# Graph-attention scores computed on quarters of TensorE and summed by VectorE, instead of on halves of TensorE

## The chip, the cores and the metric

The kernel runs on one NeuronCore of one Trainium2 chip. The metric is the device time of one execution in microseconds (us). TensorE (PE in the profile) multiplies matrices, VectorE (DVE), ScalarE (ACT) and GpSimd (POOL) work on elements, and SyncE (SP) issues most of the transfers. PEld is TensorE's loading of weights, which runs beside its products.

## The reference, cut to what matters

There are 128 graphs of 64 nodes with 384 features. For each graph the scores of all node pairs are computed, masked where `adj` has no edge, and normalised by a softmax; with these weights the rows are averaged, go through two dense layers, and are added to the input, and each row is normalised.

```python
hi_t = jnp.einsum('bid,de->bie', h, W1_w[:HID])[:, :, None, :] + jnp.einsum('bijd,de->bije', dep_emb, W1_w[HID:]) + W1_b
hj_t = jnp.einsum('bjd,de->bje', h, W2_w[:HID])[:, None, :, :] + jnp.einsum('bijd,de->bije', dep_emb, W2_w[HID:]) + W2_b
relevance = jnp.sum(hi_t * hj_t, axis=-1)
masked = jnp.where(adj, relevance, NEG)
A = jax.nn.softmax(masked, axis=2)
aggregated = jnp.einsum('bij,bjd->bid', A, h_syn)
h_syn = jax.nn.relu(aggregated @ gcn_w + gcn_b)
return h_syn @ Wo_w + Wo_b          # then x = layernorm(x + this)
```

Where all entries of `adj` are 0 or 1, as here, the score of nodes i and j is a product of two 384-long vectors plus a term of the row.

## The kernel before, in words

The 8192 nodes are cut into 16 groups (`GROUPS`; `LAST` is 15) of 512 tokens. A group is 4 pairs of graphs (`PAIRS`), and a pair fills the 128 partitions: graph e of a pair has partitions 64e to 64e+63. The 384 features are 3 blocks of 128 (`C`). Each engine has its own program, written by hand; `run` executes `body(g, par)` for g = 0 and 1, then in a loop for 2 to 13, then for 14 and 15. The engines wait for each other through counted semaphores alone, and each works strictly in the order of its program. PSUM has 8 banks, given out by hand.

TensorE's `body(g)` does, in this order:

- `mix(g - 1)`: the weighted sums of group g-1, 48 products on 64x64 quarters of the array, into banks 4 to 7. It waits for the turned weights `at_sb` (`at_ready`, from VectorE) and until ScalarE has read the latest projections out of PSUM (`gt_ready`). Its middle is marked by `mix_part`.
- `score_stage(g)`: the scores, 24 products per group, each with all 128 rows of the array and 64 of its columns (graph e on column half e), three blocks c accumulated into bank 0.
- `gemm(g - 1)`: the first dense layer, 27 products of 128x512 into three banks (`GEMM_BANK`), each value in a high and a low part. It waits for the split input (`zlo`) and for the bank to be read (`added`).
- `proj(g + 1)`: the projection for the next scores, again 27 products of 128x512.
- `out(g - 1, q)`, q = 0 to 3: the second dense layer, 9 products of 128x384 for each pair. The first waits for all three low parts of the hidden layer, `hslo`, and in group 1 also for `wo_lo`, which GpSimd computes once.

VectorE's `body(g)` does: `low_z(g - 1)` (six subtractions that give `z_lo`, after ScalarE's `z_hi`); then the score stage: `rel` from the scores in PSUM, the row term `srow` and `adj_sb`, the addition of `neg_sb`, and `nmax`, the negated row maximum; then `most` (`adj_max`). It waits for ScalarE's exponentials (`weigh`, which waits for `nmax`), and continues with `rsum`, `weights`, `turn` (`at_sb`, which releases `at_ready`), `row_products` of the next group (`onehot`, `xu_row`), `normalise` of group g-2, `low_hidden(g - 1)` (three operations that give `hs_lo` and release `hslo`), and `residual(g - 1, q)`, which reads the second layer out of PSUM (`added`).

GpSimd does the large element-wise work of SBUF alone: `split_x` (`xt_lo`), `bias_x` (`y_sb`), and once `wo_lo`, for which it waits until `row_products` of group 2 are there (`xu_ready`). ScalarE's `body(g)` is `split_z`, in group 1 `row_terms` and `split_x`, `weigh`, `hidden`, `split_x` of a later group, and `project_out`.

Of the kernel before, what the change touches and what calls it, by code (L numbers as in the profile page):

```python
# [41 lines left out]
ALU = mybir.AluOpType  # L42
# [4 lines left out]
P = 128  # L47
# [6 lines left out]
def gnn_layernorm_kernel(nc, x, x_t, adj, adj_t, edge, biases, w1_t, w2_t, gcn_w, wo_w, wo_b, out):  # L54
    HID, TOKENS = x_t.shape
    NODES = adj.shape[2]
    EDIM, NTYPES = edge.shape[0], edge.shape[1] - 2 * HID
    C = HID // P
    PAIRS = 4
    GT = PAIRS * P  # L60
    GROUPS = TOKENS // GT
    HALVES = PAIRS // 2
    MIX = PAIRS * NODES
    LAST = GROUPS - 1
# [14 lines left out]
    with ExitStack() as ctx:  # L79
# [3 lines left out]
        def sem(name):  # L83
            return ctx.enter_context(nc.semaphore(name))
# [34 lines left out]
        xt_sb = sb("xt_sb", [P, 2, C, GT])  # L119
# [52 lines left out]
        banks = ctx.enter_context(nc.psum_tensor("banks", [P, 8, 512], F32))  # L172
        bank = [banks[:, i, :] for i in range(8)]
        score = bank[0]
        GEMM_BANK = [bank[2], bank[3], bank[1]]
        PROJ_BANK = bank[4:7]
        PROJ1_BANK = bank[1:4]
        M_BANK = bank[4:7]
        U_BANK = bank[7]
        C_BANK = bank[3]  # L180
# [67 lines left out]
        mix_part = sem("mix_part")  # L248
        xu_ready = sem("xu_ready")
        srow_ready = sem("srow_ready")  # L250
        masked = sem("masked")
        expd = sem("expd")
        normed = sem("normed")
# [59 lines left out]
        def out_bank(g, q):  # L313

            if static(g, LAST - 2) and HALVES <= q:
                return bank[(3, 2)[q - HALVES]]
            if static(g, LAST - 1):
                return bank[(3, 1, 6, 7)[q]]
            if static(g, LAST):
                return bank[(3, 1, 2, 4)[q]]  # L320
            return bank[(1, 2, 3, 1)[q]]

        def gemm_bank(g):

            return [bank[2], bank[4], bank[5]] if static(g, LAST) else GEMM_BANK

        def column(g, q):

# [32 lines left out]
        def static(g, n):  # L361

            return isinstance(g, int) and g == n
# [96 lines left out]
        def _(pe):  # L460
# [6 lines left out]
            def proj(g, par, into=PROJ_BANK, parts=range(C * C)):  # L467

                for part in parts:
                    f, c = part // C, part % C  # L470
                    fs = slice(f * P, (f + 1) * P)
                    mm = three(into[f][:, 0:GT], m_hi[:, c, fs], m_lo[:, c, fs],
                               xt_hi[:, par, c, :], xt_lo[:, par, c, :], c == 0, c == C - 1)
                    if c == C - 1:
                        mm.then_inc(proj_mm, 1)

            def score_stage(g, par):
                pe.wait_ge(gt_ready, C * (g + 1))
                for n in range(PAIRS):
                    for c in range(C):  # L480
                        for e in range(2):
                            ts = slice(n * P + e * NODES, n * P + (e + 1) * NODES)
                            mm = pe.matmul(score[e * NODES:(e + 1) * NODES, n * NODES:(n + 1) * NODES],  # L483
                                           gt_sb[:, c, ts], xt_sb[:, par, c, ts], start=(c == 0), stop=(c == C - 1))
                mm.then_inc(score_mm, 1)

            def gemm(g):

                for f in range(C):
                    fs = slice(f * P, (f + 1) * P)  # L490
                    if static(g, LAST):
                        pe.wait_ge(added, PAIRS * (g - 1))
                    elif not (static(g, 0) or static(g, LAST - 1) and f == C - 1):
                        pe.wait_ge(added, PAIRS * (g - 1) + f + 2)
                    for n, c in enumerate(BLOCKS):
                        if f == 0:
                            pe.wait_ge(zlo, C * g + n + 1)
                        mm = three(gemm_bank(g)[f][:, 0:GT], gcn_hi[:, c, fs], gcn_lo[:, c, fs],
                                   z_hi[:, c, :], z_lo[:, c, :], n == 0, n == C - 1)
                    mm.then_inc(gemm_mm, 1)  # L500

            def mix(g, par):
                pe.wait_ge(at_ready, g + 1)
                if static(g, 0):
                    pe.wait_ge(gt_ready, C)
                elif not static(g, LAST):
                    pe.wait_ge(gt_ready, C * (g + 2))
                pe.sem_inc(mix_begun, 1)

                def pass_of(*streams):  # L510

                    for q in range(PAIRS):
                        for f, h in streams:
                            at = MIX * (f % 2)
                            rows = slice(h * NODES, (h + 1) * NODES)
                            for e in range(2):
                                mm = pe.matmul(  # L517
                                    bank[MIX_BANK[h][f]][e * NODES:(e + 1) * NODES, at + q * NODES:at + (q + 1) * NODES],
                                    x_sb[rows, par, q, f * P + e * NODES:f * P + (e + 1) * NODES],
                                    at_sb[rows, q * NODES:(q + 1) * NODES], start=True, stop=True)  # L520
                    return mm

                pass_of((0, 1), (0, 0))
                pass_of((1, 1), (1, 0)).then_inc(mix_part, 1)
                pass_of((2, 1), (2, 0)).then_inc(mix_mm, 1)
# [81 lines left out]
            def body(g, par):  # L607

                if not static(g, 0):
                    mix(g - 1, 1 - par)  # L610
                score_stage(g, par)
                if static(g, 0):
                    proj(1, 1, PROJ1_BANK, range(2, C * C))
                    return
                if static(g, 1):
                    pe.wait_ge(gcn_lo_ready, 1)
                gemm(g - 1)
                if static(g, LAST):
                    out(g - 2, 3)
                    mix(g, par)  # L620
                    out(g - 1, 0)
                    out(g - 1, 1)
                    gemm(g)
                    out(g - 1, 2)
                    out(g - 1, 3)
                    for q in range(PAIRS):
                        out(g, q)
                    return
                pe.wait_ge(xlo, g + 2)
                proj(g + 1, 1 - par)  # L630
                if static(g, 1):
                    pe.wait_ge(wo_lo_ready, 1)
                for q in range(PAIRS - 1 if static(g, LAST - 1) else PAIRS):
                    out(g - 1, q)
# [191 lines left out]
        def _(dve):  # L826
# [118 lines left out]
            def body(g, par):  # L945

                if not static(g, 0):
                    low_z(g - 1)
                dve.wait_ge(score_mm, g + 1)
                dve.wait_ge(negm, g + 1)  # L950
                dve.wait_ge(srow_ready, g + 1)
                for q in range(PAIRS):
                    a = dve.scalar_tensor_tensor(rel[:, q, :], score[:, q * NODES:(q + 1) * NODES],  # L953
                                                 srow[:, q:q + 1], adj_sb[:, par, q, :], ALU.add, ALU.mult)
                a.then_inc(masked, 1)
                dve.wait_ge(masked, 3 * g + 1)
                dve.tensor_tensor(rel[:], rel[:], neg_sb[:, par], ALU.add).then_inc(masked, 1)
                dve.wait_ge(masked, 3 * g + 2)
# [283 lines left out]
```

## Time and profile before

| what | value |
|---|---|
| median of 3 runs | 376.71 us (376.21 to 377.17) |
| the profiled execution's own time | 376.19 us |
| its span, first to last instruction | 374.3 us |
| mean granted TensorE clock | 0.998 of full speed |
| PE busy | 364.7 us, 97% of the span |
| DVE busy | 274.8 us, 73% |
| ACT busy | 180.1 us, 48% |
| POOL busy | 144.9 us, 39% |

All times below are microseconds from the span's start. In a row of the timeline the first number is the start, the second the duration, then come engine, line, operation, output<-inputs, shapes and the number of instructions in it; square brackets give the idle time of that engine just before, and what ended it. An fp32 product shows as two records on TensorE, so 24 products are x48. Matmul durations include the pipeline, so neighbours overlap, and the distance between two starts is the price of one.

### The profile page before, as it was taken

How to read it: one execution, taken by the hardware profiler on the slowest of the kernel's cores; microseconds unless marked ns; L12 is line 12 of the kernel's file. 1: busy time of each engine (PE TensorE's matmuls, PEld its weight loads, DVE VectorE, ACT ScalarE, POOL GpSimd, SP SyncE). 2: the span in 40 equal slices, each digit the busy share in tenths (PEclk: the TensorE clock that was granted, in tenths of full speed). 3: DMA queues.
4: the chain of work that ended last, by engine and by line, in shares of the span. 5: the costliest groups of instructions: out<-in, count | busy, mean ns of one | idle time of the engine just before them, and what ended most of it. 6: DMA issues, size and time to landing. Idle time of an engine off the chain costs nothing.

```text
span 374.3 us, 9938 instructions
## 1 busy us (share of the span) xinstructions
PE 364.7 (97%) x3827; PEld 316.7 (85%) x3827; DVE 274.8 (73%) x773; ACT 180.1 (48%) x371; POOL 144.9 (39%) x108
## 2 busy tenths in 40 slices
PE   8999999999999999999999999999999999999994
PEld 5787798988889898888989888898988989897893
DVE  1559768687786868788686878868677785867856
ACT  1566717165272715527272552727255282616552
POOL 1603461716134171613517152351715235142714
PEclk9999999999999999999999999999999999999999
DMA  7995005564443556344354534435553443550033
GB/s 236 353 328 170 28 10 176 168 185 132 146 158 92 174 168 182 120 156 158 88 179 168 182 113 154 165 89 179 168 179 101 162 161 100 168 170 4 17 112 129
DMA packets 43268, 55.48 MB, mean 148 GB/s; under 512 B 10352, under 2 KB 37488, under 8 KB 43248
## 3 DMA queue, kind: packets, MB, share of 16 engines
q1 hardware_dynamic: 42448, 54.30, 45.8%
q10 hardware_dynamic: 800, 0.90, 0.7%
q8 instruction: 13, 0.21, 0.2%
q14 instruction: 7, 0.06, 0.1%
HBM read 42.61 MB, written 12.58 MB: 147 GB/s over the span
## 4 chain that ended last, share of the span: by engine, by line
PE 89%; DVE 7%; DMA 1%; POOL 1%; ACT 1%; issue 1%; POOLq 0%
PE banks L463 25%; PE banks L465 24%; PE banks L464 24%; PE banks L517 6%; PE banks L483 6%; PE banks L557 2%; DVE onehot L833 1%; DVE z_lo L923 1%; DMA w1t_sb<-in_w_t_dram 1%; DVE adj_max L916 1%; DVE at_sb L941 1%; POOL wo_lo L1173 1%; ACT prob L752 1%; DVE rel L953 1%; DVE at_sb L936 0%
## 5 line engine op out<-in xcount | busy, mean ns | idle before, releaser
L1128 POOL TENSOR_TENSOR y_sb<-y_sb,wob_sb 128x1536 f32<-128x1536 f32 x15 | 52.8, 3519 | 84.7 <-DVE y_sb L864 73.8
L764 ACT CAST z_hi<-banks 128x512 fp32r<-128x512 f32 x48 | 26.6, 588 | 99.3 <-PE banks L517 93.9
L842 DVE TENSOR_TENSOR y_sb<-banks,y_sb 128x384 f32<-128x384 f32 x60 | 33.4, 556 | 48.7 <-PE banks L465 44.3
L463 PE MATMUL banks<-wo_hi,hs_hi 128*128 128x384 f32 x180 | 60.7, 337 | 1.6 <-DVE xt_lo L930 1.2
L464 PE MATMUL banks<-wo_lo,hs_hi 128*128 128x384 f32 x180 | 60.5, 336 | 0.0
L465 PE MATMUL banks<-wo_hi,hs_lo 128*128 128x384 f32 x180 | 60.5, 336 | 0.0
L463 PE MATMUL banks<-z_hi,gcn_hi 128*128 128x512 f32 x144 | 58.3, 405 | 0.0
L463 PE MATMUL banks<-xt_hi,m_hi 128*128 128x512 f32 x144 | 57.2, 397 | 0.0
L465 PE MATMUL banks<-xt_hi,m_lo 128*128 128x512 f32 x144 | 56.4, 392 | 0.0
L465 PE MATMUL banks<-z_hi,gcn_lo 128*128 128x512 f32 x144 | 56.4, 392 | 0.0
L464 PE MATMUL banks<-z_lo,gcn_hi 128*128 128x512 f32 x144 | 56.1, 389 | 0.0
L464 PE MATMUL banks<-xt_lo,m_hi 128*128 128x512 f32 x144 | 56.0, 389 | 0.0
L1116 POOL TENSOR_TENSOR xt_lo<-xt_sb,xt_hi 128x1536 fp32r<-128x1536 f32 x15 | 53.1, 3538 | 7.2 <-ACT xt_hi L707 7.2
L713 ACT ACTIVATE gt_sb<-banks,r_sb 128x512 f32<-128x512 f32 x48 | 32.8, 686 | 32.6 <-PE banks L465 32.6
L1136 POOL TENSOR_TENSOR veps<-mv,eps_sb 128x4 f32<-128x4 f32 (+2 forms) x20 | 4.1, 206 | 107.4 <-DVE mv L856 107.4
L923 DVE TENSOR_TENSOR z_lo<-banks,z_hi 128x256 fp32r<-128x256 f32 x96 | 34.6, 418 | 8.3 <-ACT z_hi L764 8.3
L752 ACT ACTIVATE prob<-rel,nmax 128x64 f32<-128x64 f32 x64 | 21.5, 337 | 36.2 <-DVE nmax L959 36.2
L463 PEld LDWEIGHTS banks<-wo_hi,hs_hi 128*128 128x128 f32 x180 | 33.8, 188 | 3.0 <-DVE xt_lo L930 1.6
L847 DVE BATCH_NORM_STATS2 stats<-y_sb 128x6 f32<-128x384 f32 x60 | 33.6, 560 | 2.1
L930 DVE SCALAR_TENSOR_TENSOR hs_lo<-banks,ngb_sb,less_sb 128x512 fp32r<-128x512 f32 x45 | 31.2, 746 | 4.7 <-ACT less_sb L777 4.7
L464 PEld LDWEIGHTS banks<-wo_lo,hs_hi 128*128 128x128 f32 x180 | 33.8, 188 | 0.5
L465 PEld LDWEIGHTS banks<-wo_hi,hs_lo 128*128 128x128 f32 x180 | 33.8, 188 | 0.0
(103 smaller groups left out, 612.6 us busy)
## 6 DMA issues: line engine op xcount, KB each, us to landing
x_sb<-in_x_dram SPq DMA_DIRECT2D x16, 768.0 KB, 4.6
xt_sb<-in_x_t_dram SPq DMA_DIRECT2D x15, 768.0 KB, 6.5
y_sb<-in_x_dram SPq DMA_DIRECT2D x15, 768.0 KB, 4.5
out_dram<-y_sb SPq DMA_DIRECT2D x30, 384.0 KB, 2.5
adj_sb<-in_adj_dram SPq DMA_DIRECT2D x32, 64.0 KB, 3.1
xt_sb<-in_x_t_dram SPq DMA_DIRECT2D x2, 384.0 KB, 6.6
xt_sb<-in_x_dram SPq DMA_DIRECT2D x1, 768.0 KB, 6.1
w2t_sb<-in_w_t_dram SPq DMA_DIRECT2D x3, 192.0 KB, 4.5
```

The lines of the kernel that those rows point to most:

```text
L463: pe.matmul(acc, a_hi, b_hi, start=first, stop=False)
L464: pe.matmul(acc, a_hi, b_lo, start=False, stop=False)
L465: return pe.matmul(acc, a_lo, b_hi, start=False, stop=last)
L713: act.activation(gt_sb[:, f, :], of[f][:, 0:GT], ACT.Identity, bias=r_sb[:, f:f + 1]).then_inc(gt_ready, 1)
L752: a = act.activation(prob[:, q, :], rel[:, q, :], ACT.Exp, bias=nmax[:, q:q + 1], accum_out=psum_row[:, q:q + 1])
L764: act.copy(by_graph(z_hi[:, f, :]), mixed(f)).then_inc(zhi, 1)
L842: dve.tensor_tensor(y_home(g, slot)[:, q, :], out_bank(g, q)[:, 0:HID], y_home(g, slot)[:, q, :], ALU.add).then_inc(added, 1)
L847: dve.bn_stats(stats[:, q, :], y_home(g, slot)[:, q, :]).then_inc(statd, 1)
L923: a = dve.tensor_tensor(by_graph(z_lo[:, f, :])[:, h], mixed(f)[:, h], by_graph(f32(z_hi[:, f, :]))[:, h], ALU.subtract)
L930: dve.scalar_tensor_tensor(hs_home(g)[1][:, f, :], gemm_bank(g)[f][:, 0:GT], ngb_sb[:, f:f + 1], less_sb[:, f, :], ALU.max, ALU.subtract). ...
L1116: pool.tensor_tensor(xt_lo[:, slot], xt_sb[:, slot], f32(xt_hi[:, slot]), ALU.subtract).then_inc(xlo, 1)
L1128: pool.tensor_tensor(y_home(g, slot), y_home(g, slot), wob_sb[:].rearrange("p (o n) -> p o n", o=1).to_broadcast([P, PAIRS, HID]), ALU.add ...
```

## The change

`score_stage` now puts each block of 128 features onto two row halves (r) of the array: 48 products per group on 64x64 quarters, the shape of `mix`. Row half 0 accumulates into bank 0, row half 1 into bank 2 (`SCORE_BANK`). VectorE adds the two: `rel` = bank 0 + `srow`, then `rel` = bank 2 + `rel`, then `rel` times `adj_sb`, each on all 256 columns, in place of four operations of 64 columns that did all in one from bank 0. The new semaphore `summed` counts the two additions. As bank 2 is now used by the scores, the dense layer's banks go in another order, its third part waits for `summed`, the first two wait for other counts of `added`, `mix` waits for the bank's last reader (`added`) and takes over the wait for `gt_ready` from `score_stage` (which keeps it in groups 0 and 1), and in group 0 the last third of the projection waits for `summed`. The banks of the last groups' outputs are rearranged to match.

```diff
-        GEMM_BANK = [bank[2], bank[3], bank[1]]
+        SCORE_BANK = bank[0], bank[2]
+        GEMM_BANK = [bank[3], bank[1], bank[2]]
         PROJ_BANK = bank[4:7]
-        PROJ1_BANK = bank[1:4]
+        PROJ1_BANK = [bank[1], bank[3], bank[2]]
...
             if static(g, LAST - 2) and HALVES <= q:
-                return bank[(3, 2)[q - HALVES]]
+                return bank[3]
             if static(g, LAST - 1):
-                return bank[(3, 1, 6, 7)[q]]
+                return bank[(1, 2, 6, 7)[q]]
             if static(g, LAST):
-                return bank[(3, 1, 2, 4)[q]]
+                return bank[(1, 2, 3, 4)[q]]
...
             def score_stage(g, par):
-                pe.wait_ge(gt_ready, C * (g + 1))
+                if static(g, 0) or static(g, 1):
+                    pe.wait_ge(gt_ready, C * (g + 1))
                 for n in range(PAIRS):
                     for c in range(C):
-                        for e in range(2):
-                            ts = slice(n * P + e * NODES, n * P + (e + 1) * NODES)
-                            mm = pe.matmul(score[e * NODES:(e + 1) * NODES, n * NODES:(n + 1) * NODES],
-                                           gt_sb[:, c, ts], xt_sb[:, par, c, ts], start=(c == 0), stop=(c == C - 1))
+                        for r in range(2):
+                            rows = slice(r * NODES, (r + 1) * NODES)
+                            for e in range(2):
+                                ts = slice(n * P + e * NODES, n * P + (e + 1) * NODES)
+                                mm = pe.matmul(SCORE_BANK[r][e * NODES:(e + 1) * NODES, n * NODES:(n + 1) * NODES],
+                                               gt_sb[rows, c, ts], xt_sb[rows, par, c, ts],
+                                               start=(c == 0), stop=(c == C - 1))
                 mm.then_inc(score_mm, 1)
...
-                    elif not (static(g, 0) or static(g, LAST - 1) and f == C - 1):
-                        pe.wait_ge(added, PAIRS * (g - 1) + f + 2)
+                    elif f == C - 1:
+                        pe.wait_ge(summed, 2 * (g + 2))
+                    elif not (static(g, 0) or static(g, LAST - 1) and f == 1):
+                        pe.wait_ge(added, PAIRS * (g - 1) + f + 3)
...
                 elif not static(g, LAST):
                     pe.wait_ge(gt_ready, C * (g + 2))
+                    pe.wait_ge(added, PAIRS * (g - 1) + 2)
...
                 if static(g, 0):
-                    proj(1, 1, PROJ1_BANK, range(2, C * C))
+                    proj(1, 1, PROJ1_BANK, range(2, 2 * C))
+                    pe.wait_ge(summed, 2)
+                    proj(1, 1, PROJ1_BANK, range(2 * C, C * C))
...
                 dve.wait_ge(score_mm, g + 1)
+                dve.wait_ge(srow_ready, g + 1)
+                first, second = (b[:, 0:MIX].rearrange("p (q n) -> p q n", n=NODES) for b in SCORE_BANK)
+                dve.tensor_tensor(rel[:], first, srow[:].rearrange("p (q o) -> p q o", o=1).to_broadcast([P, PAIRS, NODES]),
+                                  ALU.add).then_inc(summed, 1)
+                dve.wait_ge(summed, 2 * g + 1)
+                dve.tensor_tensor(rel[:], second, rel[:], ALU.add).then_inc(summed, 1)
+                dve.wait_ge(summed, 2 * g + 2)
                 dve.wait_ge(negm, g + 1)
-                dve.wait_ge(srow_ready, g + 1)
-                for q in range(PAIRS):
-                    a = dve.scalar_tensor_tensor(rel[:, q, :], score[:, q * NODES:(q + 1) * NODES],
-                                                 srow[:, q:q + 1], adj_sb[:, par, q, :], ALU.add, ALU.mult)
-                a.then_inc(masked, 1)
+                dve.tensor_tensor(rel[:], rel[:], adj_sb[:, par], ALU.mult).then_inc(masked, 1)
```

VectorE's program in the looped body, from the end of `low_z` to `most`, before (a wait in brackets stands ahead of its row; REGISTER_ALU and ISA rows only count and wait):

```order
L923 TENSOR_TENSOR z_lo<-banks,z_hi 128x4x64 [waits zhi]
L923 TENSOR_TENSOR z_lo<-banks,z_hi 128x4x64
L949 REGISTER_ALU
L953 SCALAR_TENSOR_TENSOR rel<-banks,srow,adj_sb 128x64 [waits srow_ready,negm,score_mm]
L953 SCALAR_TENSOR_TENSOR rel<-banks,srow,adj_sb 128x64 x3
L956 ISA
L957 TENSOR_TENSOR rel<-rel,neg_sb 128x256 [waits masked]
L958 REGISTER_ALU
L959 TENSOR_REDUCE nmax<-rel 128x4 [waits masked]
L961 REGISTER_ALU
L916 TENSOR_TENSOR adj_max<-adj_max,adj_sb 128x256 [waits adjmax,statd]
```

The same place in the changed kernel (its lines are 11 to 14 higher here):

```order
L934 TENSOR_TENSOR z_lo<-banks,z_hi 128x4x64
L960 REGISTER_ALU
L963 TENSOR_TENSOR rel<-banks,srow 128x256 [waits srow_ready,score_mm]
L965 ISA
L966 TENSOR_TENSOR rel<-banks,rel 128x256 [waits summed]
L967 REGISTER_ALU
L969 TENSOR_TENSOR rel<-rel,adj_sb 128x256 [waits negm,summed]
L970 ISA
L971 TENSOR_TENSOR rel<-rel,neg_sb 128x256 [waits masked]
L972 REGISTER_ALU
L973 TENSOR_REDUCE nmax<-rel 128x4 [waits masked]
L927 TENSOR_TENSOR adj_max<-adj_max,adj_sb 128x256 [waits adjmax,statd]
```

Nothing changes places; four rows of 64 columns that do not wait for each other became three of 256 columns that each wait for the one ahead.

TensorE's program at the head of the looped body, before:

```order
L507 ISA [waits at_ready]
L517 MATMUL banks<-at_sb,x_sb 64x64 [waits gt_ready]
L517 MATMUL banks<-at_sb,x_sb 64x64 x47
L483 MATMUL banks<-xt_sb,gt_sb 64x64 [waits gt_ready]
L483 MATMUL banks<-xt_sb,gt_sb 64x64 x23
L494 ISA
L497 ISA [waits added]
L463 MATMUL banks<-z_hi,gcn_hi 128x512 [waits zlo]
```

The same place in the changed kernel:

```order
L515 ISA [waits at_ready]
L516 ISA [waits gt_ready]
L526 MATMUL banks<-at_sb,x_sb 64x64 [waits added]
L526 MATMUL banks<-at_sb,x_sb 64x64 x47
L488 MATMUL banks<-xt_sb,gt_sb 64x64 x48
L502 REGISTER_ALU
L505 ISA [waits added]
L465 MATMUL banks<-z_hi,gcn_hi 128x512 [waits zlo]
```

The score products are twice as many and follow `mix` without a wait of their own; the wait for `added` stands ahead of `mix` now as well.

## Rows read from the trace of the kernel before

**Rows 1.** The chain that ended last, one group: start, duration, what.

```profile
205.84 1.56 PE banks L517 x96
207.40 1.55 PE banks L483 x48
...
227.76 1.56 PE banks L517 x96
```

**Rows 2.** Timeline of the same group (body 8), all engines.

```profile
205.50 0.34 PE L465 MATMUL banks<-wo_hi,hs_lo 128*128 128x384 f32 x1
205.77 1.63 PE L517 MATMUL banks<-at_sb,x_sb 64*64 64x64 f32 x96
...
207.62 2.17 DVE L923 TENSOR_TENSOR z_lo<-banks,z_hi 128x256 fp32r<-128x256 f32 x6 [0.58 <-ACT z_hi L764]
...
209.70 0.85 DVE L953 SCALAR_TENSOR_TENSOR rel<-banks,srow,adj_sb 128x64 f32<-128x64 f32 x4
...
210.58 0.43 DVE L957 TENSOR_TENSOR rel<-rel,neg_sb 128x256 f32<-128x256 f32 x1
...
211.04 0.42 DVE L959 TENSOR_REDUCE nmax<-rel 128x4 f32<-128x256 f32 x1
...
211.50 0.35 ACT L752 ACTIVATE prob<-rel,nmax 128x64 f32<-128x64 f32 x1 [2.50 <-DVE nmax L959]
...
212.97 0.18 DVE L970 RECIPROCAL rsum<-psum_row 128x4 f32<-128x4 f32 x1 [0.88 <-ACT prob L752]
...
218.88 2.06 DVE L930 SCALAR_TENSOR_TENSOR hs_lo<-banks,ngb_sb,less_sb 128x512 fp32r<-128x512 f32 x3
...
221.36 0.34 PE L463 MATMUL banks<-wo_hi,hs_hi 128*128 128x384 f32 x1
```

**Rows 3.** Timeline of the last body, where TensorE does wait for `hslo`.

```profile
345.70 2.06 DVE L930 SCALAR_TENSOR_TENSOR xt_lo<-banks,ngb_sb,less_sb 128x512 fp32r<-128x512 f32 x3
...
346.49 0.44 PE L463 MATMUL banks<-wo_hi,hs_hi 128*128 128x384 f32 x1 [1.19 <-DVE xt_lo L930]
...
346.77 0.34 PE L464 MATMUL banks<-wo_lo,hs_hi 128*128 128x384 f32 x1
...
346.95 0.34 PE L465 MATMUL banks<-wo_hi,hs_lo 128*128 128x384 f32 x1
```

**Rows 4.** Single lines of the program: count, duration in ns min/median/max, first and last start.

```profile
L483 PE MATMUL banks<-xt_sb,gt_sb x768: 222/222/270, 22.2 to 338.7; 128*64 128x64 f32 x192
L923 DVE TENSOR_TENSOR z_lo<-banks,z_hi x96: 414/416/425, 31.5 to 351.9; 128x256 fp32r<-128x256 f32 x96
L916 DVE TENSOR_TENSOR adj_max<-adj_max,adj_sb x16: 416/417/3292, 25.5 to 341.3; 128x256 int32<-128x256 int32 x16
```

**Rows 5.** Timeline of the first two groups.

```profile
28.28 1.25 DVE L941 STREAM_TRANSPOSE at_sb<-weights 32x128 f32<-32x128 f32 x4
...
29.68 1.63 PE L517 MATMUL banks<-at_sb,x_sb 64*64 64x64 f32 x96 [0.86 <-ACT gt_sb L713]
...
33.59 0.85 DVE L953 SCALAR_TENSOR_TENSOR rel<-banks,srow,adj_sb 128x64 f32<-128x64 f32 x4
...
34.48 0.42 DVE L957 TENSOR_TENSOR rel<-rel,neg_sb 128x256 f32<-128x256 f32 x1
...
34.53 3.75 POOL L1116 TENSOR_TENSOR xt_lo<-xt_sb,xt_hi 128x1536 fp32r<-128x1536 f32 x1 [6.21 <-ACT xt_hi L707]
...
35.28 3.29 DVE L916 TENSOR_TENSOR adj_max<-adj_max,adj_sb 128x256 int32<-128x256 int32 x1
...
38.49 0.16 DVE L970 RECIPROCAL rsum<-psum_row 128x4 f32<-128x4 f32 x1
...
40.91 0.56 DVE L833 SCALAR_TENSOR_TENSOR onehot<-x_sb,u_row 128x384 f32<-128x384 f32 x1
```

**Rows 6.** Timeline around the end of group 1's projection.

```profile
43.15 2.69 POOL L1173 TENSOR_TENSOR wo_lo<-wo_sb,wo_hi 128x1152 fp32r<-128x1152 f32 x1 [4.87 <-DVE onehot L833]
...
45.03 0.40 PE L465 MATMUL banks<-xt_hi,m_lo 128*128 128x512 f32 x1
...
45.89 0.44 PE L463 MATMUL banks<-wo_hi,hs_hi 128*128 128x384 f32 x1 [0.46 <-POOL wo_lo L1173]
```

More of the change, by code:

```diff
@@ L250, in gnn_layernorm_kernel @@
         srow_ready = sem("srow_ready")
+        summed = sem("summed")
         masked = sem("masked")
@@ L315, in out_bank @@
             if static(g, LAST - 2) and HALVES <= q:
-                return bank[(3, 2)[q - HALVES]]
+                return bank[3]
             if static(g, LAST - 1):
-                return bank[(3, 1, 6, 7)[q]]
+                return bank[(1, 2, 6, 7)[q]]
             if static(g, LAST):
-                return bank[(3, 1, 2, 4)[q]]
+                return bank[(1, 2, 3, 4)[q]]
             return bank[(1, 2, 3, 1)[q]]
         def gemm_bank(g):
-            return [bank[2], bank[4], bank[5]] if static(g, LAST) else GEMM_BANK
+            return [bank[3], bank[4], bank[5]] if static(g, LAST) else GEMM_BANK
         def column(g, q):
```

## The prediction, made before the changed kernel was run

> **What bounds the kernel now.** I read the table first: TensorE is busy for 97% of the span and VectorE for 73%, so at first sight only TensorE's time counts. The chain that ended last agrees. One group takes 227.76 - 205.84 = 21.92 us, in which `mix` has 1.56 us for 96 records and the scores 1.55 us for 48 [rows 1]. But the share of busy time hides how close VectorE is. In the timeline of one group I followed the way from `mix` to the first product of `out`, which waits for `hslo`. VectorE waits for `z_hi` and starts `z_lo` at 207.62; from there `rel`, two more operations, ScalarE's exponentials at 211.50 and VectorE's work from 212.97 follow each other without a pause that anything outside ends, up to `hs_lo`, which runs from 218.88 to 220.94. The product that needs it starts at 221.36 [rows 2]. How late may `hs_lo` be? The last body shows a case where TensorE waits for it: three operations in 2.06 us from 345.70, the first of about 0.74 us (their starts lie 0.66 us apart), so it ends at 346.44; the product starts at 346.49, and the next follows after 0.28 us instead of 0.18, so the wait costs some 0.05 + 0.10 us behind the release [rows 3]. In the middle groups that gives 220.94 + 0.15 = 221.09 against 221.36: VectorE's slack is 0.27 us per group, no more.
>
> **The change part by part.** *TensorE's products.* Four quarters replace two halves. The price stands in the trace, since `mix` uses exactly these quarters: 96 records in 1.56 us, and 48 on halves in 1.55 us [rows 1]. The changed stage has 96 records, so I take 1.55 us again; the number of columns streamed through each part of the array stays. What can be gained is the change of shape between `mix` and scores. Where TensorE goes from whole array to quarters, the start comes 0.27 us after the last one instead of 0.18 [rows 2, 3]; and the first records of the score stage take 270 ns, not 222 [rows 4]. So a removed change of shape is worth 0.09 to 0.14 us, times 15 groups (group 0's scores follow products on the whole array) 1.4 to 2.1 us.
>
> The Trainium skill says the same in TensorEngine Tiling (Array Packing), Tiling Modes: going to another tiling mode, as against another tile of the same mode, drains the engine. By that rule alone the sum would be a gain of about 2 us, and the time some 374 us; it is the first rival below.
>
> This saving does not shorten the way just followed: that starts in `mix` (`mix_part` lies in its middle), and `rel` starts at 209.70, when `z_lo` ends and not when the scores do, at 208.95 [rows 1, 2]. So it is kept only as long as TensorE, not VectorE, decides when `out` starts.
>
> *VectorE's additions.* Removed: four operations, 210.58 - 209.70 = 0.88 us from the first to the next stage. Added: three of 256 columns, each waiting for the one before. The nearest rows are `rel` plus `neg_sb`, 211.04 - 210.58 = 0.46 us from start to start with its wait [rows 2], and 0.416 us for an operation of the same size out of PSUM [rows 4], with the same gap 0.45. The sum is 3 x 0.46 - 0.88 = 0.50 us later; from below 3 x 0.42 - 0.88 = 0.38 (no gap at all). The multiplication by integers is costed as the integer operation of `adj_max`, 0.417 [rows 4].
>
> *Middle groups.* `hs_lo` ends at 220.94 + 0.50, and TensorE's product starts 0.15 behind: 221.59, that is 0.23 us later than 221.36. The next `mix` is later by as much, and VectorE's way starts from it again, so each group pays. Groups 1 to 13, whose `out` follows a full body 2 to 14, make 13 x 0.23 = 3.0 us (bounds: 0.11 to 0.27, 1.4 to 3.5). In the last body TensorE already idles 1.19 us for `hs_lo` [rows 3]; there all of 0.50 counts.
>
> *First two groups.* In group 0 nothing covers VectorE: `at_sb` ends at 28.28 + 1.25 = 29.53 and `mix` starts at 29.68 after 0.86 us of idle time [rows 5]. All later starts move by 0.50. In group 1 GpSimd comes in. Before, `rel` plus `neg_sb`, with both inputs in SBUF, starts at 34.48, and GpSimd's subtraction at 34.53 runs 3.75 us, to 38.28. The next VectorE operation with both inputs in SBUF, `adj_max`, takes 3.29 us there, to 38.57, and 0.417 in the median [rows 4, 5]: it stands until GpSimd is done. That hurt little, as ScalarE's exponentials were running. Now GpSimd's operation moves by the same 0.50 as everything behind `mix`, to 35.03, and `rel` to 34.09, but the addition of `neg_sb` to 34.09 + 1.38 = 35.47. It comes 0.4 us after GpSimd instead of 0.05 ahead, and stands until 39.07. `nmax` starts at 39.10, the exponentials at 39.56 (0.46 later, as before), `rsum` 1.47 us behind them [rows 2] at 41.03: 2.54 later than 38.49. The multiplication by `adj_sb` would start at 35.01, within 0.02 us of GpSimd; if it is caught too, another 0.25 to 0.5 is lost. Behind it stand `weights`, `at_sb` and `row_products`, then `wo_lo`, 2.24 us after `row_products` start [rows 5, 6]. TensorE waits 0.46 us for `wo_lo` already [rows 6], so the 2.54 arrives whole (the first 0.50 included).
>
> The Trainium skill has this in SBUF — State Buffer, Who interferes with whom: an operation of VectorE with two SBUF inputs contends with one of GpSimd that reads SBUF, and the one that issues first holds the port for its whole run. The `adj_max` of 3.29 us agrees.
>
> *The other waits.* The third part of the dense layer waits for both additions, done at 209.70 + 0.92 = 210.62; it starts 18 products of 0.23 us (54 of them between 208.95 and 221.36) behind the scores, at 213.1. 2.5 us cover it. `mix` waits for the read of `out`'s second result, whose products end some 3.1 us before (18 of 0.17), the read being one short VectorE operation. In group 0 the projection's last third comes four parts of 0.69 behind the scores, 2.7 us, against 0.92. All cost nothing. The wait for `added` in the first two parts is older than `zlo` in VectorE's order.
>
> *Sum.* 2.54 + 3.0 + 0.50 = 6.0 us on the profiled execution's 376.19: 382.2. That execution is 0.52 below the median of the runs shown and 0.02 below their fastest, so I forecast half of this above it: 382.4.
>
> **The rivals.** *TensorE's saving decides, faster.* If the three operations together took under 0.88 + 0.27 = 1.15 us, `out` would not wait, and the 1.4 to 2.1 us would stay: about 374.5. For it speaks only that the chain shows TensorE alone. Against it: 0.38 us each would be needed, and the trace has nothing of that size under 0.416 [rows 4]. Chance 0.06. *The stretches cancel, no change*: VectorE partly hidden, no stop in group 1, +0.5 in two places, less the saving: about 376.5; 0.04. *No stop behind GpSimd*: if the addition slips in ahead of it, as 0.05 us decided before, group 1 keeps `adj_max`'s stop as it is, the first term falls to 0.50, and the time is 380.3; against it stands the 0.44 us by which the addition is now too late. 0.13. *Quarters do not run side by side when they accumulate*: `mix` writes each result once, the scores add three blocks into one place. If two of four ran at a time, the stage would take 3.1 us, 1.5 more per group, of which the 0.23 is no longer extra: some 397. `mix`'s pace speaks against it; 0.04. The forecast itself has 0.73.
>
> **How the numbers follow.** The forecast's own range is 380.5 to 383.8: the middle groups give 1.4 to 3.5, the stop up to 0.5 more, the median half a microsecond. With the rival without a stop the range goes to 379.7; above, a TensorE idle for 2.7 us in group 1 is something the trace does not show, so I leave it at 384.0. 0.3% is 1.1 us, about what a measurement of this kernel can tell from no change. Faster 0.06, same 0.04, slower 0.90.
>
> **What would show it.** In the changed profile: 96 score records in about 1.45 to 1.55 us; VectorE's three operations 1.38 us from start to start of the next stage; a new wait of TensorE for `hs_lo` in 13 groups, and a period of 22.15 us; in group 1 the addition of `neg_sb` at 3.6 us instead of 0.42, and a wait for `wo_lo` of some 2.7 us. I am wrong if TensorE's first product of `out` still follows the projection without a pause, or if the addition in group 1 takes its usual time.

## The result and the profile after

The changed kernel took 388.45 us in the median of 5 runs (387.63 to 388.83), beside 376.71 us (376.21 to 377.17) for the kernel before: 1.0309 times its time, interval 1.0298 to 1.032. The prediction was 382.4 us with a range of 379.7 to 384.0. The direction and the terms that it names hold; about as much again came from places that it left out. One execution of a later experiment (TensorE kept busy) took 1282.39 us and is left out of every comparison. The profiled execution's own time is 388.54 us, 12.35 above that of before.

Three lines of the page: busy time of TensorE's products, the granted clock in 40 slices, and the queue that brings instructions.

```profile
PE 368.7 (95%) x4595; PEld 317.1 (82%) x4595; DVE 282.2 (73%) x757; ACT 180.3 (47%) x371; POOL 144.6 (37%) x108
PEclk9999989999999999999999999999999999999998
q8 instruction: 15, 0.25, 0.3%
```

The 768 records more (before: x3827; 384 products of two records each) were expected. Not expected were the dip of the clock in the sixth slice and the 15 packets of code; the page of before has 13 and no dip.

The timeline of one middle group, which answers to [rows 1, 2], with a later `mix` behind it:

```profile
212.90 1.63 PE L526 MATMUL banks<-at_sb,x_sb 64*64 64x64 f32 x96
214.34 1.58 PE L488 MATMUL banks<-xt_sb,gt_sb 64*64 64x64 f32 x96
215.85 0.51 PE L465 MATMUL banks<-z_hi,gcn_hi 128*128 128x512 f32 x1
...
216.82 0.41 DVE L963 TENSOR_TENSOR rel<-banks,srow 128x256 f32<-128x256 f32 x1
217.27 0.42 DVE L966 TENSOR_TENSOR rel<-banks,rel 128x256 f32<-128x256 f32 x1
217.73 0.43 DVE L969 TENSOR_TENSOR rel<-rel,adj_sb 128x256 f32<-128x256 f32 x1
218.19 0.42 DVE L971 TENSOR_TENSOR rel<-rel,neg_sb 128x256 f32<-128x256 f32 x1
226.50 2.06 DVE L941 SCALAR_TENSOR_TENSOR hs_lo<-banks,ngb_sb,less_sb 128x512 fp32r<-128x512 f32 x3
228.61 0.19 PEld L465 LDWEIGHTS banks<-wo_hi,hs_hi 128*128 128x128 f32 x1 [0.54 <-DVE hs_lo L941]
235.06 1.63 PE L526 MATMUL banks<-at_sb,x_sb 64*64 64x64 f32 x96
```

The three operations ahead of the addition of `neg_sb` take 218.19 - 216.82 = 1.37 us. `hs_lo` starts 13.60 us behind `mix`, against 13.11 before, and TensorE's load now waits for it. The group takes 235.06 - 212.90 = 22.16 us instead of 21.92. All this is as predicted (1.38, a new wait, 22.15). The removed change of shape shows too: the scores start 1.44 us behind `mix` instead of 1.56, and the saving is lost in the wait for `hs_lo`.

The first two groups, which answer to [rows 5, 6]:

```profile
22.64 1.15 ACT L756 CAST wo_hi<-wo_sb 128x1152 fp32r<-128x1152 f32 x1 [0.88 <-DMA wo_sb<-in_wo_w_dram]
24.09 0.42 DVE L963 TENSOR_TENSOR rel<-banks,srow 128x256 f32<-128x256 f32 x1 [2.74 <-PE banks L488]
30.40 1.63 PE L526 MATMUL banks<-at_sb,x_sb 64*64 64x64 f32 x96 [1.42 <-DVE at_sb L952]
35.26 3.77 POOL L1130 TENSOR_TENSOR xt_lo<-xt_sb,xt_hi 128x1536 fp32r<-128x1536 f32 x1 [6.21 <-ACT xt_hi L718]
35.68 3.62 DVE L971 TENSOR_TENSOR rel<-rel,neg_sb 128x256 f32<-128x256 f32 x1
...
45.94 2.62 POOL L1187 TENSOR_TENSOR wo_lo<-wo_sb,wo_hi 128x1152 fp32r<-128x1152 f32 x1 [6.92 <-DVE onehot L844]
48.61 0.45 PE L465 MATMUL banks<-wo_hi,hs_hi 128*128 128x384 f32 x1 [2.60 <-POOL wo_lo L1187]
```

The addition of `neg_sb` starts 0.42 us behind GpSimd's subtraction, takes 3.62 us instead of 0.42, and TensorE waits 2.60 us for `wo_lo` (2.7 expected). `mix` of group 0 starts 0.72 us later than before: 0.48 from VectorE, and 0.24 because `rel` started later (24.09, 23.85 before). Of the 0.24, 0.16 are the scores of group 0, which started at 22.34 instead of 22.18; the rest are ScalarE's row terms, which ended behind the scores because `wo_sb` landed later.

What the prediction had no term for stands first in the chain that ended last, at three places (start, duration, what; "issue" is time in which the engine waited for nothing that the profile shows):

```profile
49.75 0.17 PE banks L467
...
50.19 0.32 PE banks L466
...
53.07 0.32 PE banks L466
53.39 0.18 PE banks L467
...
80.41 1.28 PE banks L488 x87
81.69 1.28 issue
...
325.32 0.82 PE banks L488 x55
326.13 1.28 issue
327.41 0.85 PE banks L488 x41
```

From 1.25 us behind the end of its idle of 2.60 us, TensorE runs its products in 0.32 us instead of 0.17, for 3.4 us: the granted clock is at the lower of its two levels, 1.2 instead of 2.4 GHz. And in groups 3 and 14 the score products stop in the middle, after 87 and 55 of 96 records, with nothing to wait for. Group 15 has a third stop, hidden behind VectorE.

Last, the transfers: the last store (KB, us from issue to landing), and a packet of code in the 1.5 us ahead of and into the stop of group 3.

```profile
out_dram<-xt_sb ACTq DMA_DIRECT2D x1, 192.0 KB, 4.2
...
q8 instruction: 1, 0.02, 5.1%
```

The last store took 2.0 us before, and the program ends behind it.

| where | after less before, us | predicted |
|---|---|---|
| VectorE in group 0 and the stop in group 1 | 0.48 + 1.99 | 2.54 |
| 13 periods up to group 14 | 13 x 0.24 = 3.1 | 3.0 |
| last body | 0.51 | 0.50 |
| score products stopping, groups 3 and 14 | 1.16 + 1.14 = 2.3 | none |
| lower clock in group 1 | 1.57 | none |
| last store and what ends behind it | 2.2 | none |
| later start of `rel` in group 0 | 0.24 | none |

The sum is 12.4, the growth of the span (386.7 - 374.3).

### The profile page after: what moved, and what is told of

The parts are those of the page before. It is cut to its first block, busy times and chain, and to the rows that moved or that the text cites. A ratio compares the mean times of both kernels' runs of the same rounds, so it can differ in the third digit from the quotient of the medians.

```text
span 386.7 us, 11500 instructions
## 1 busy us (share of the span) xinstructions
PE 368.7 (95%) x4595; PEld 317.1 (82%) x4595; DVE 282.2 (73%) x757; ACT 180.3 (47%) x371; POOL 144.6 (37%) x108
## 4 chain that ended last, share of the span: by engine, by line
PE 41%; DVE 39%; ACT 7%; issue 5%; DMA 3%; SPq 2%; POOL 1%; DVEq 0%; POOLq 0%
PE banks L465 12%; PE banks L466 11%; PE banks L467 11%; DVE onehot L844 7%; DVE hs_lo L941 6%; DVE z_lo L934 6%; PE banks L526 5%; ACT prob L763 5%; DVE y_sb L875 4%; DVE at_sb L952 4%; DMA wo_sb<-in_wo_w_dram 3%; DVE rel L971 2%; ACT z_hi L775 2%; DVE at_sb L947 2%; DVE rel L969 2%
## 5 line engine op out<-in xcount | busy, mean ns | idle before, releaser
L465 PE MATMUL banks<-wo_hi,hs_hi 128*128 128x384 f32 x180 | 62.5, 347 | 4.6 <-POOL wo_lo L1187 2.6
## 6 DMA issues: line engine op xcount, KB each, us to landing
out_dram<-y_sb SPq DMA_DIRECT2D x30, 384.0 KB, 2.5
xt_sb<-in_x_t_dram SPq DMA_DIRECT2D x2, 384.0 KB, 6.5
```

Of the source, the lines that this page charges most:

```text
L465: pe.matmul(acc, a_hi, b_hi, start=first, stop=False)
```

## The experiments

My theory: the named terms are right, and the new ones are, first, TensorE waiting for its own instructions, since quarters double the instructions of the stage while the stage takes no longer; second, the lower clock after the idle in group 1; third, a fetch of code that meets the last store. The rival for the first is a stop that belongs to the quarters themselves (two row halves, two banks); for the last, that a store at the end simply varies.

**Halves, but three operations.** The products as before, VectorE as after; the second operand is a cleared part of bank 0. The edit, cut, against the changed kernel:

```diff
-        SCORE_BANK = bank[0], bank[2]
...
+            dve.memset(score[:, MIX:2 * MIX], 0.0)
...
-                first, second = (b[:, 0:MIX].rearrange("p (q n) -> p q n", n=NODES) for b in SCORE_BANK)
+                first, second = (score[:, at:at + MIX].rearrange("p (q n) -> p q n", n=NODES) for at in (0, MIX))
...
```

> TensorE as in the kernel before (halves, bank 0 alone, no new waits); VectorE with the three operations of the change, the second of which adds columns of bank 0 that hold zeros. So only VectorE's part of the change is there. Theory 1 (VectorE's loop, the stop behind GpSimd, and a TensorE that is slow after its long idle time; late code belongs to the doubled score products alone): the period of the middle groups is 22.16 us, the addition of neg_sb in group 1 takes 3.6 us, TensorE idles some 2.5 us before the first out and then needs 0.32 us per product for some 10 products; no idle time of the score products; 376.7 + 2.5 + 1.6 + 3.1 + 0.5 = 384.4 us. Rival (all stalls and the slow products come with the quarters): no slow products, 382.8 us. If the last transfer of 4.2 us belongs to VectorE's part, 2 us more.

Measured: 383.91 us (383.33 to 384.58), 1.0202 of before (1.0183 to 1.0221). Middle groups take 22.17 us, no score stage stops, there are 13 packets of code, and the last store lands as before:

```profile
q8 instruction: 13, 0.21, 0.2%
...
out_dram<-xt_sb ACTq DMA_DIRECT2D x1, 192.0 KB, 2.2
```

So VectorE's operations alone carry the predicted terms, and the stops and the late store belong to the quarters. The span is 7.5 us longer than before, not 6.0: 1.6 us of it lie ahead of `mix` of group 0, where 0.5 was expected (how much that start varies, the kernel before taken again shows below). Against what I expected, the clock stayed up in group 1, behind an idle of 2.46 us.

**Quarters, but VectorE as before.** The four operations read bank 0 alone; the second half of each block's features is left out of the scores. The edit, cut; where TensorE waited for `summed`, it waits for the first `masked`:

```diff
...
-                dve.tensor_tensor(rel[:], first, srow[:].rearrange("p (q o) -> p q o", o=1).to_broadcast([P, PAIRS, NODES]),
-                                  ALU.add).then_inc(summed, 1)
...
-                dve.tensor_tensor(rel[:], second, rel[:], ALU.add).then_inc(summed, 1)
...
-                dve.tensor_tensor(rel[:], rel[:], adj_sb[:, par], ALU.mult).then_inc(masked, 1)
+                for q in range(PAIRS):
+                    a = dve.scalar_tensor_tensor(rel[:, q, :], score[:, q * NODES:(q + 1) * NODES],
+                                                 srow[:, q:q + 1], adj_sb[:, par, q, :], ALU.add, ALU.mult)
+                a.then_inc(masked, 1)
...
```

> TensorE as in the changed kernel (quarters, both banks, banks in the new order), VectorE as before: four operations that read bank 0 alone, so the second half of the features is left out of the scores; where the change waits for summed, TensorE waits for VectorE's first operation on the same scores. Only TensorE's part of the change is there. Theory 1 (quarters save the change of shape, 0.1 to 0.15 us per group, and lose time where their doubled code is run for the first time): middle groups at 21.77 us, idle time of 0.5 to 1.3 us inside the score products of two or three of the groups 3, 14 and 15 and in no other, no stop and no slow products in group 1; 376.7 - 2.0 + 2.6 = 377.3 us, 379.4 if the slow last transfer comes with it. Rival (quarters as such are slower, or the new waits of TensorE cost time in every group): a period above 21.92 us, 378 us or more, idle time in all groups.

Measured: 379.74 us (379.29 to 380.53), 1.0084 (1.0068 to 1.0101). From its chain:

```profile
207.22 1.56 PE banks L525 x96
229.00 1.56 PE banks L525 x96
...
76.44 1.28 PE banks L487 x87
77.72 1.37 issue
...
317.72 0.82 PE banks L487 x55
318.54 0.99 issue
```

A group takes 21.78 to 21.80 us, 0.13 less than before: the removed change of shape is worth what the prediction gave it (0.09 to 0.14) once VectorE doesn't decide. The Trainium skill's TensorEngine Tiling (Array Packing), Tiling Modes, by which going to another mode drains the engine, agrees. The stops at records 87 and 55 are there without VectorE's new operations, and the last store takes 4.3 us.

**GpSimd's subtraction behind the row maximum, group 1.**

```diff
                 mask(g + 1, 1 - par)
+                if static(g, 0):
+                    pool.wait_ge(masked, 3 * (g + 2))
```

> The changed kernel; GpSimd's xt_lo of group 2 waits until VectorE has the row maxima of group 1. Theory 1: the addition of neg_sb takes 0.42 us in group 1 again, TensorE's wait for wo_lo falls from 2.6 to about 0.5 us, so the following out products run at 0.17 us each: 2.0 and 1.6 us less, 388.45 - 3.6 = 384.9 us; stalls in groups 3, 14 and 15 unchanged. Rival (the slow products of group 1 have another cause than the idle time): they stay at 0.32, 386.4 us. Rival (the loss of group 1 is taken up later): no change, 388.4.

Measured: 385.23 us (385.09 to 386.67), 1.0233 (1.0216 to 1.025). In its timeline the addition takes its usual time, and TensorE waits as little for `wo_lo` as before [rows 6]:

```profile
31.62 2.84 PE L526 MATMUL banks<-at_sb,x_sb 64*64 64x64 f32 x96 [2.25 <-DVE at_sb L952]
...
37.84 0.42 DVE L971 TENSOR_TENSOR rel<-rel,neg_sb 128x256 f32<-128x256 f32 x1
38.80 3.63 POOL L1130 TENSOR_TENSOR xt_lo<-xt_sb,xt_hi 128x1536 fp32r<-128x1536 f32 x1 [8.53 <-DVE nmax L973]
...
49.47 0.44 PE L465 MATMUL banks<-wo_hi,hs_hi 128*128 128x384 f32 x1 [0.51 <-POOL wo_lo L1187]
```

So the stop was GpSimd's, as predicted; the Trainium skill's SBUF — State Buffer, Who interferes with whom, by which an operation of VectorE with two inputs in SBUF contends with one of GpSimd that reads SBUF, agrees with 3.62 against 0.42 us. This profiled execution, the slowest of the four, had its lower clock in another place: `mix` of group 0 took 2.84 us instead of 1.63, after 2.25 us of idle.

**TensorE kept busy in group 1.** Two products that nobody reads, ahead of the wait for `wo_lo`.

```diff
                 if static(g, 1):
+                    for _ in range(2):
+                        pe.matmul(score[:, 0:GT], zero[:].to_broadcast([P, P]), zero[:].to_broadcast([P, GT]),
+                                  start=True, stop=True)
                     pe.wait_ge(wo_lo_ready, 1)
```

> The changed kernel; in group 1, ahead of the wait for wo_lo, TensorE multiplies zeros twice (512 columns in fp32) into bank 0, which nobody reads then. Theory 1 (TensorE's clock falls to half after 2.6 us without products): with about 0.9 us of idle time left it does not fall, all out products of group 1 take 0.17 us, 388.45 - 1.6 = 386.9 us, everything else as in the changed kernel; the stalls of groups 3, 14 and 15 come some 6 records earlier, as 12 instructions are ahead of them. Rival (the products of group 1 are slow for another reason, such as wo_lo or its port): unchanged at 388.4.

Measured: 386.69 us, 1.0273 (1.0252 to 1.0293). The idle ahead of the first product of `out` is 0.90 us, the clock stays at its upper level, and group 1 takes 24.66 us instead of 26.22: 1.56 less, the price read above. (The changed kernel taken again, below, keeps its clock up without this edit, so this profile alone does not show the idle to be the cause.) The eight instructions also moved the stops, to records 83 (group 3) and 32 (group 15), four records earlier. The one in group 15 is now 1.05 us long instead of 0.55 and no longer hidden: the last body takes 13.47 us instead of 13.04. The one in group 14 is gone; code was asked for there 0.36 us ahead of `mix`, not 1.08 us behind its start, and why is open.

**Code moved.** 30 small products instead, 60 records and their loads.

```diff
                 if static(g, 1):
+                    for n in range(30):
+                        e = n % 2 * NODES
+                        pe.matmul(score[e:e + NODES, 0:SQUARE], zero[0:NODES].to_broadcast([NODES, NODES]),
+                                  zero[0:NODES].to_broadcast([NODES, SQUARE]), start=True, stop=True)
                     pe.wait_ge(wo_lo_ready, 1)
```

> The changed kernel with 30 small products of zeros (64x64, 32 columns, fp32: 120 instructions) in TensorE's idle time of group 1, ahead of the wait for wo_lo; nobody reads their result. All code behind them lies 120 instructions further on. Theory 1 (the idle times inside the score products are waits for code, which comes in blocks of 16 KB as the queue q8 shows; the places seen fit a block every 256 instructions): the idle time at record 87 of group 3 is gone, those at 55 of group 14 and 36 of group 15 are gone or elsewhere, and a new one can stand near record 59 of group 2. The period of the loop's later passes stays 22.16 us. With the shorter idle time before out the half-speed products of group 1 are probably gone as well, so 384.5 to 387 us. Rival (the idle times come from a wait of these groups for another engine): the same three at the same records as in the changed kernel.

Measured: 386.15 us (385.3 to 387.34), 1.0244 (1.0222 to 1.0266). The chain has one stop left, in a group that had none before:

```profile
55.81 1.56 PE banks L526 x96
57.37 0.93 PE banks L488 x59
58.30 0.90 issue
59.20 0.80 PE banks L488 x37
```

Group 2 takes 23.01 us, groups 3 and 14 have their usual 22.15 and 20.59. The score stages themselves are untouched, so the stop follows the place in the code (record 59 of group 2, as expected) and not the quarters as such: the rival falls. That the place alone is not enough either, the kernel before shows. There a packet of code starts at 53.94, as the score stage of group 2 starts, just as in group 3 of the changed kernel, and the 48 records run through:

```profile
53.96 1.55 PE banks L483 x48
...
q8 instruction: 1, 0.02, 5.6%
```

In this profile the clock fell in the last body, behind an idle of 1.80 us ahead of `out`, and the body takes 13.82 us (window, us, busy time of PE, PEld, DVE, ACT and POOL, granted clock, transfers):

```profile
355.10:358.40 3.30, 3.30 (x62) 2.86 (x65) 1.81 (x6) 0.00 (x0) 3.25 (x1) 0.50 0.00 0
```

**Quarters with two operations, halves with one.** Both leave out the term of the row and the multiplication by `adj`, which don't change a softmax over the unmasked entries, and add `neg_sb` straight to the scores out of PSUM. The new lines, first of the quarters (against the changed kernel), then of the halves (against the kernel before); the lines that they replace are cut:

```diff
...
+                dve.tensor_tensor(rel[:], first, neg_sb[:, par], ALU.add).then_inc(masked, 1)
                 dve.wait_ge(masked, 3 * g + 1)
+                dve.tensor_tensor(rel[:], second, rel[:], ALU.add).then_inc(masked, 1)
```

```diff
...
+                dve.tensor_tensor(rel[:], score[:, 0:MIX].rearrange("p (q n) -> p q n", n=NODES), neg_sb[:, par],
+                                  ALU.add).then_inc(masked, 2)
```

> The changed kernel's TensorE; VectorE computes rel = bank 0 + neg_sb, then rel = bank 2 + rel, and the maximum. The row term srow and the multiplication by adj_sb are left out: the first is constant along the softmax's axis and the second only matters where 1e9 has been subtracted, so the result is the same within rounding. VectorE is 0.89 + 0.46 - 0.92 = 0.43 us faster than before instead of 0.49 slower. Theory 1: TensorE decides again, middle groups at 21.79 us; no stop in group 1 as both additions read PSUM; the waits for code of 1.5, 1.1 and 0.3 us in groups 3, 14, 15 and the late last store of 2 us stay, as TensorE's code is as long: 376.4 - 1.6 + 2.9 + 2.0 - 0.5 - 0.4 = 378.8 us. Rival (VectorE's additions alone made the change slow): 374 us.

> The kernel before, whose VectorE computes rel = bank 0 + neg_sb in one operation of 256 columns and then the maximum; srow and the multiplication by adj_sb are left out as above, the result is the same within rounding. VectorE's stage is 0.89 us shorter. Theory 1 (VectorE has slack in the middle groups before, and none at both ends): the period stays 21.92 us; the last body's wait for hs_lo falls from 1.19 to about 0.3 us, and the wait of 0.46 us for wo_lo goes: 376.4 - 1.35 = 375.0 us, no waits for code, last store as before. Rival (VectorE's time counts in every group): 13 x 0.89 less, 364 us.

Measured: quarters 378.42 us (377.75 to 379.18), 1.0051 (1.0034 to 1.0067); halves 374.55 us (374.06 to 375.34), 0.9946 (0.9929 to 0.9963), which beats both kernels. `mix` and scores of a middle group, of the quarters and then of the halves:

```profile
205.79 1.63 PE L525 MATMUL banks<-at_sb,x_sb 64*64 64x64 f32 x96
207.24 1.58 PE L487 MATMUL banks<-xt_sb,gt_sb 64*64 64x64 f32 x96
```

```profile
204.87 1.63 PE L517 MATMUL banks<-at_sb,x_sb 64*64 64x64 f32 x96
206.43 1.62 PE L483 MATMUL banks<-xt_sb,gt_sb 128*64 128x64 f32 x48
```

The quarters win 0.13 us in each of 11 middle groups (21.79 against 21.92), 1.4 in all. They still lose 3.9 in the time, 3.4 between the two profiles: groups 3 and 14 stop again (23.15 and 21.53 us against 21.92 and 20.36, 2.4 together), group 1 takes 0.44 longer and the last body 0.54, each with one VectorE operation more, and the end behind the last `mix` 1.4. So the rival of the prediction by which TensorE's saving decides would not have come out faster here even with VectorE out of the way.

**The branch behind the last store.** TensorE ends with a conditional block that is not executed here; it now waits for the stores first. After and before were profiled again beside it.

```diff
+            for slot in range(2):
+                pe.wait_ge(stored[slot], 1 + 16 * STORES[slot])
             with pe.If(is_general(pe)):
```

> The changed kernel; at its end TensorE waits until all stores have landed before it branches over the code for other inputs. Theory 1 (the last store of 192 KB lands after 3.6 to 4.3 us instead of 2.0 to 2.2 because TensorE's code block of 16 KB, asked for at this branch, is read about 1.1 us behind the store's issue, in the middle of it; in the kernel before it is read 1.7 us behind, when the store is through): the store lands after some 2.0 us, and the code block is read afterwards; the time falls by as much as TensorE's end allows, between 0 and 2 us below 388.45. Rival (the store is late for another reason, as the longer program on TensorE or the order of the stores): it lands after about 4 us as in the changed kernel.

> The changed kernel once more, for what differs from execution to execution. Idle times of the score products at records 87, 55 and 36 of groups 3, 14, 15 again, periods 22.16 us, the last store after about 4 us; where wo_sb lands, and whether and when TensorE's clock falls to half for some 3.4 us, can differ.

> The kernel before once more: no idle time of the score products, periods 21.92 us, the last store after about 2 us; where wo_sb lands can differ, and moves the start of the first mix only when it is more than some 0.4 us later than in the first profile.

Measured: 387.01 us (386.25 to 387.55), 1.0283 (1.0266 to 1.03). The row of the last store in its profile, and in that of after taken again:

```profile
out_dram<-xt_sb ACTq DMA_DIRECT2D x1, 192.0 KB, 1.9
```

```profile
out_dram<-xt_sb ACTq DMA_DIRECT2D x1, 192.0 KB, 4.1
```

In after again the fetch of code starts 1.06 us after the store's issue and the store's packets end at 3.6; with the branch behind the store they end at 1.5, and the fetch starts at 3.9. The meeting of the two is the cause. Only part comes back in the time: the span ends 384.4 - 380.83 = 3.6 us behind the issue, against 385.2 - 380.62 = 4.6, as the branch is now last (2.5 in before). Before has a fetch there as well, 1.7 us after the issue, when the packets are through. Every profile divides the same way: with halves the fetch starts 1.70 to 1.71 us after the issue and the store lands on time, with quarters and the branch where it was it starts 1.05 to 1.10 us after, and the store is late. Why the larger program asks for it 0.65 us sooner I could not settle.

After again took 387.04 us, before again 377.36. In the latter `rel` and `mix` of group 0 start 1.01 us later than in the first profile (`mix` at 30.69), though `wo_sb` landed within 0.04 us of its time there; I had expected a later start only with a later `wo_sb`. So a shift of up to 1 us ahead of this `mix` says nothing of the change. This execution of after has the same idle of 2.60 us in group 1, but its clock stayed up, as two windows of it show (us, busy time of each engine, granted clock, transfers), beside the same stretches of after above:

```profile
46.50:49.10 2.60, 0.01 (x1) 0.01 (x1) 1.67 (x3) 2.50 (x5) 2.60 (x2) 1.00 0.01 3
49.10:54.00 4.90, 4.90 (x28) 4.90 (x29) 1.45 (x3) 0.00 (x0) 4.90 (x3) 1.00 0.00 0
```

```profile
45.94:48.60 2.66, 0.07 (x1) 0.00 (x0) 1.75 (x3) 2.57 (x5) 2.66 (x2) 1.00 0.01 3
48.60:53.40 4.80, 4.79 (x18) 4.79 (x19) 1.12 (x2) 0.00 (x0) 4.80 (x3) 0.64 0.00 0
```

Its group 1 takes 24.65 us, 1.57 less than in the first profile. The branch's profile, too, has an idle of 2.60 us there and no fall. So the idle does not force the fall. That it is what makes it possible is not shown, but the profiles speak for it: of six with an idle of 1.8 us or more behind the first score stage and ahead of the last product, three have a fall of the clock within 1.3 us of its end (2.60 us here, 2.25 in the third experiment, 1.80 with the code moved), and of the six without such an idle none has.

## Why the prediction was right and wrong

- *VectorE's additions and middle groups*: right. 1.37 us for three operations against 1.38, 0.24 us per group against 0.23, and the halves with three operations gave them alone.
- *First two groups*: right. 0.48 + 1.99 against 2.54, by the stop that was named; without GpSimd's subtraction there it was gone.
- *Last body*: right, 0.51 against 0.50.
- *The removed change of shape*: right in size (0.13 us) and in its fate, as VectorE decided.
- *TensorE's products*, "I take 1.55 us again": this step failed. The price per record holds, but I counted only time in the array and not the 768 more records and their 768 loads, which had to be fetched. `mix` and scores are now 192 records in 3.0 us. In groups 3 and 14 code was asked for inside or just ahead of the stage (from 80.27 and 324.77), and TensorE ran out of instructions 1.4 us later, until 82.98 and 327.41. Between the start of a fetch and the next product lie 2.6 to 2.7 us there, 2.3 in the stop of group 15 and in that of the moved code. A dense layer with 0.23 us for a product hides that. No stop appears in groups 4 to 13, which repeat a loop's code: the queue brings no packet for TensorE between 84.59 and 324.77. The cost is 2.3 us here, 1.7 to 2.0 in the three other profiles with stops at these records and VectorE as changed. The Trainium skill, Runtime: NRT & Kernel Launch, Instruction fetch mechanics, has code fetched in blocks of 16 KiB ahead of time, with the crossing of a block "mostly hidden". The queue agrees (15 packets, 0.25 MB), and most are hidden; two of them here cost over 1.1 us each.
- *"A TensorE idle for 2.7 us in group 1 is something the trace does not show, so I leave it at 384.0"*: this step failed, and it was avoidable. I had derived the idle myself and then gave its unknown consequence no room above. It cost 1.57 us in the profiled execution and nothing in another. Most executions behind the median probably paid it: the mean granted clock of the five was 0.989 to 0.993 in four, among them the profiled one, and 0.996 in the fastest (387.63 us), as in after again, which had no fall; the kernel before never showed less than 0.995.
- *The sum* ended with the last body. The 2.2 us behind the last store have no term in it: this step failed too, as the end was put at nothing without a reason. Neither has the 0.24 by which `rel` of group 0 started later; that is chance, as the same start moved by 1.01 us between the two profiles of before.

The rivals without a stop in group 1, with stretches that cancel, and with quarters that do not run side by side are all refuted by rows above (3.62 us; 22.16 us; 96 records in 215.85 - 214.34 = 1.51 us). The price of the last one was also a little low: 13 times 1.27 us on 382.2 is nearer 399 than 397. What stays open is what decides between one execution's lower clock and another's upper one, and why the last fetch comes sooner.

## What to carry to other kernels

Count instructions as well as time in the array: a stage that is split into twice as many small products needs its code twice as fast, and where code runs for the first time, TensorE can stop for it in the middle. A wait that an estimate creates on the bounding engine needs a second look, at what follows on its clock, and its unknown side belongs in the range. And where engines are nearly level, price each operation's distance to the one it may be caught behind: 0.4 us later cost 2 us here.

## What the runs showed of the hardware that was not expected

- TensorE's fall to 1.2 GHz after an idle is not certain: 2.60 us of idle in group 1 was followed by 3.4 us at the lower level in one execution of the same kernel and not in another; 2.25 us ahead of `mix` of group 0 in the third experiment and 1.80 us in the last body with the code moved were followed by it, 2.46 us in group 1 of the halves with three operations was not.
- Stops of TensorE for code are placed by the count of instructions: eight instructions more moved two of them by four records, 120 more moved the one in group 3 to record 59 of group 2, as expected. A fetch as a score stage starts stopped 96 records and not 48.
- A fetch of 16 KB of code on the queue of instructions, 1.1 us after the issue of a 192 KB store, let the store land after 3.6 to 4.3 us instead of 1.9 to 2.2.
